# A fused two-layer block: value projections placed ahead of the first maxima, and the order of scores, maxima and layouts behind them

## The reference, cut to what matters

```
q, k, v = heads(h @ Wq + bq), heads(h @ Wk + bk), heads(h @ Wv + bv)
y  = softmax(causal(q @ k.T * scale)) @ v
qc, kc, vc = heads(h @ Wcq + bcq), heads(c @ Wck + bck), heads(c @ Wcv + bcv)
y += softmax(qc @ kc.T * scale) @ vc
x  = x + tanh(g) * (y @ Wp + bp)        # h is the layer norm of x, c the second input
```

## Time and profile before

| | |
|---|---|
| median of 3 runs | 335.41 us |
| the three runs | 332.91, 335.91, 335.41 us |
| span of the profiled execution | 337.6 us |
| mean granted clock of PE | 0.995 of full |
| PE, DVE, ACT, POOL busy | 312.9, 220.8, 194.1, 115.7 us |
| instructions | 7474 |

### The profile page before, as it was taken

One profiled execution on the slowest core, in us unless ns is written; L12 is line 12 of the kernel. 1 busy time (PEld: TensorE's weight loads), 2 busy tenths in 40 slices (PEclk: granted clock), 3 DMA queues, 4 the chain that ended last, 5 costly groups with the idle time before them and its releaser, 6 DMA issues.

```text
span 337.6 us, 7474 instructions
## 1 busy us (share of the span) xinstructions
PE 312.9 (93%) x2891; PEld 189.6 (56%) x2891; DVE 220.8 (65%) x532; ACT 194.1 (57%) x410; POOL 115.7 (34%) x200
## 2 busy tenths in 40 slices
PE   8998969989999999899977999999996899999995
PEld 3545733334443434344666677777794357776665
DVE  4998798888989889676242052333321956779665
ACT  3468588978888889787266733323336265512221
POOL 6476732327334333231775003444442211110000
PEclk9999999999999999999997999999999999999999
DMA  7855995940437006240441580000002200000101
GB/s 174 199 110 160 175 213 132 209 90 10 153 110 209 5 5 188 70 124 2 109 157 35 133 212 10 21 18 19 22 12 70 71 0 2 1 2 0 31 3 31
DMA packets 35827, 27.83 MB, mean 82 GB/s; under 512 B 5627, under 2 KB 33070, under 8 KB 35792
## 3 DMA queue, kind: packets, MB, share of 16 engines
q1 hardware_dynamic: 33965, 25.04, 29.7%
q0 software_dynamic: 1280, 1.88, 1.7%
q10 hardware_dynamic: 547, 0.44, 0.5%
HBM read 11.89 MB, written 5.26 MB: 51 GB/s over the span
## 4 chain that ended last, share of the span: by engine, by line
PE 73%; ACT 7%; DVE 6%; issue 5%; POOL 5%; DMA 2%; SPq 0%; DVEq 0%; POOLq 0%; ACTq 0%
PE psum L1682 11%; PE psum L1876 11%; PE psum L1957 8%; PE psum L1624 5%; PE psum L1648 5%; PE psum L1945 4%; PE psum L1864 4%; ACT qk_r L948 3%; PE psum L1814 2%; POOL rows_in L797 2%; PE psum L1651 2%; PE psum L2060 2%; PE psum L2052 1%; PE psum L1575 1%; PE psum L1869 1%
## 5 line engine op out<-in xcount | busy, mean ns | idle before, releaser
L1213 DVE TENSOR_REDUCE nmax<-psum 128x2 f32<-128x1024 f32 (+2 forms) x88 | 102.0, 1216 | 11.6 <-PE psum L1624 10.3
L948 ACT ACTIVATE parts<-psum 128x512 f32<-128x512 f32 (+1 forms) x88 | 45.2, 566 | 8.6 <-PE psum L1648 7.7
L1876 PE MATMUL psum<-p_more,kcat 128*128 128x320 f32 (+2 forms) x160 | 40.2, 396 | 0.9 <-DVE p_more L1346 0.7
L819 POOL DMA_INDIRECT rows_back<-qcat,back_at x24 | 22.9, 952 | 50.3 <-ACT qcat L981 43.1
L1876 PEld LDWEIGHTS psum<-p_more,kcat 128*128 128x128 f32 x160 | 26.1, 190 | 9.1 <-issue 0.9
L1350 DVE TENSOR_TENSOR qcat<-psum,qk_r 128x320 f32<-128x320 f32 (+2 forms) x40 | 16.6, 422 | 22.1 <-ACT qk_r L989 13.5
L989 ACT ACTIVATE qk_r<-psum 128x320 f32<-128x320 f32 (+2 forms) x40 | 15.2, 384 | 24.5 <-PE psum L1876 21.5
L1682 PE MATMUL psum<-parts,v_aug 128*18 128x256 f32 (+1 forms) x352 | 28.5, 369 | 0.0
L1957 PE MATMUL psum<-h_t,kcat 128*128 128x512 f32 x60 | 28.1, 594 | 0.0
L1682 PE MATMUL psum<-qk_r,v_aug 128*18 128x256 f32 (+1 forms) x160 | 27.4, 373 | 0.0
L1648 PE MATMUL psum<-qcat,kcat 64*128 64x256 bf16 x256 | 24.7, 271 | 1.9 <-ACT p_more L948 0.8
(11 more groups left out here) (249 smaller groups left out, 630.4 us busy)
## 6 DMA issues: line engine op xcount, KB each, us to landing
kcat<-parts SPq DMA_DIRECT2D x18, 192.0 KB, 3.8
qcat<-parts SPq DMA_DIRECT2D x21, 128.0 KB, 3.6
kcat<-ones_b SPq DMA_DIRECT2D x8, 192.0 KB, 4.6
kcat<-in_L_ffn_wi_gate_dram SPq DMA_DIRECT2D x6, 256.0 KB, 4.5
kcat<-in_L_ffn_wi_up_dram SPq DMA_DIRECT2D x6, 256.0 KB, 4.8
kcat<-in_L_ffn_wo_dram SPq DMA_DIRECT2D x6, 256.0 KB, 5.0
parts<-in_L_ffn_w_dram SPq DMA_DIRECT2D x3, 512.0 KB, 5.6
rows_in<-zeros SPq DMA_DIRECT2D x1, 1290.0 KB, 5.7
```

Of the source, the lines that this page charges most:

```text
L819: pool.indirect_dma_start(out=rows_back[:, :], out_offset=bass.IndirectOffsetOnAxis(ap=back_at[0:m, e, t:t + 1], axis=0), in_=eo[0:m, e % ...
L948: act.activation(p_slots[u % NPT][:, 0:w], s2_bank(s2_place[u])[:, 0:w], ACT.Exp, scale=SCALE).then_inc(p_in, 1)
L1213: dve.tensor_reduce(dst[:, :, n * g:n * (g + 1)], src.rearrange("p (r q k) -> p r q k", r=PAR, q=n), AX.X, ALU.max, negate=True).then_inc( ...
L1876: ins = pe.matmul(gate_up_bank(i, m)[:, 0:end - first], w_t[e][:, m, f * P:(f + 1) * P], xs_t[:, e % 2, first:end], start=True, stop=True)
```

## The change

`jobs` gets the values of batches 0 and 1 directly behind `ck` of batch 1, and `N_FIRST` becomes 16. 14 jobs are left, mixed with the first units. `LEAD` becomes 17. The first turn stands two units behind its part's end, not three (`FIRST_TURN_LAG`). SP loads the value weights ahead of the layouts of batch 0, on a semaphore of their own (`in_wv`). It lays out the queries of batch 1 before it waits for the batch's keys (`lay_out_split`), six and then six transfers instead of twelve in pairs. On POOL the split of the first maxima stands ahead of both subtractions of batch 3. On ACT the high part of batch 1, the clearing of gaps in `v_aug`, the bias row `bv_wide` and the third middle split change places, the last to the end of the jobs. DVE clears bank 7 before the first unit of part 1. Of the fillers 15 go (21 behind `ck` 1 and `xt` 2 out, 6 in).

```diff
-        N_FIRST = job_at("ck", 1) + 1
-        for b in range(B):
+        ahead = jobs.index(("ck", 1)) + 1
+        jobs[ahead:ahead + 1] = [("v", 0), ("cv", 0), ("xt", 2), ("v", 1), ("cv", 1)]
+        N_FIRST = job_at("cv", 1) + 1
+        for b in range(2, B):
             jobs += [("v", b), ("cv", b)]
...
-        FIRST_TURN_LAG = 3
+        FIRST_TURN_LAG = 2
...
-        LEAD = N1 + 7
+        LEAD = N1 + 6
...
+            def lay_out_split(b):
+                sp.wait_ge(early_in, 3)
+                for dst, src in lay_out_q(b):
+                    sp.dma_start(dst, src).then_inc(cat_in[b], 16)
+                sp.wait_ge(parts_in, b + 1)
+                for dst, src in lay_out_k(b, 0, KW):
+                    sp.dma_start(dst, src).then_inc(cat_in[b], 16)
...
             pad(0)
+            sp.dma_start(w_v[:, :], a["L0_xattn_Wv"]).then_inc(in_wv, 16)
+            sp.dma_start(w_cv[0:DC, :], a["L0_xattn_Wcv"]).then_inc(in_wv, 16)
+            sp.dma_start(w_cv[DC:DC + 1, :], a["L0_xattn_bcv"].unsqueeze(0)).then_inc(in_wv, 16)
...
-            lay_out_batch(1)
+            lay_out_split(SPLIT_DVE)
...
+                if b == B - 1:
+                    split_max(0)
                 pool.tensor_tensor(qk_r[:, b % 2, cols], qk[:, b % 2, cols], parts[:, b, 0, cols],
                                    ALU.subtract).then_inc(rest_in, 1)
-                if b == B - 1:
-                    split_max(0)
...
                 if (kind, i) == ("q", 2):
+                    clear_between()
                     split_middle(1)
...
-                if (kind, i) == ("v", 2):
-                    split_middle(3)
-                if (kind, i) == ("cv", 2):
+                if (kind, i) == ("v", 0):
+                    act.wait_ge(job_act, taken_count(job_at("ck", SPLIT_DVE)))
+                    take_high(SPLIT_DVE)
+                if (kind, i) == ("ct", 3):
+                    act.wait_ge(in_w, 16 * N_IN_W)
+                    act.wait_ge(zero_in, 2)
+                    act.activation(bv_wide[:, :], zeros[:, 0:D], ACT.Identity, bias=bv_col[:, :]).then_inc(wide_in, 1)
+                if (kind, i) == ("cv", 3):
                     act.wait_ge(pad_in[0], 16 * 4)
                     act.wait_ge(s1_free, turn_at[0] + 1)
                     dst, src = max_rows(0, 1)
                     act.dma_start(dst, src).then_inc(mrow_in[0], 16)
...
+            split_middle(3)
             act.wait_ge(in_w, 16 * N_IN_W)
             act.activation(tanh_g[:, :], gates[:, :], ACT.Tanh).then_inc(tanh_in, 1)
...
-            wait_taken(dve, max(j for j in range(len(jobs)) if job_bank[j] == O_BANK))
-            dve.memset(bank(O_BANK), 0.0).then_inc(o_clear, 1)
...
             for i, u in enumerate(pass1):
+                if i == N1:
+                    wait_taken(dve, max(j for j in range(len(jobs)) if job_bank[j] == O_BANK))
+                    dve.memset(bank(O_BANK), 0.0).then_inc(o_clear, 1)
...
-            UNREAD_AFTER = {("ct", 0): (2, 7), ("bias", 0): (2, 7), ("k", 0): (5, 7), ("ct", 1): (2, 2), ("ck", 1): (12, 3),
-                            ("xt", 2): (9, 3)}
+            UNREAD_AFTER = {("ct", 0): (2, 7), ("bias", 0): (2, 7), ("k", 0): (5, 7), ("ct", 1): (2, 2), ("cv", 0): (4, 7),
+                            ("v", 1): (2, 7)}
```

More of the change, by code:

```diff
@@ L243, in flamingo_gated_kernel @@
         in_w = sem("in_w")
+        in_wv = sem("in_wv")
         wide_in = sem("wide_in")
@@ L351, in flamingo_gated_kernel @@
         job_bank = [j % 8 if j < N_FIRST else JOB_RING[(j - N_FIRST) % len(JOB_RING)] for j in range(len(jobs))]
-        N_AHEAD = 1
-        N_TO_MIX = len(jobs) - N_FIRST - N_AHEAD
         def taken_count(j):
@@ L433, in flamingo_gated_kernel @@
         N_IN_LATE = 10
-        N_IN_WCK, N_IN_WQ, N_IN_W = 2, 6, 7
+        N_IN_WCK, N_IN_WQ, N_IN_W, N_IN_WV = 2, 6, 4, 3
         UNITS1 = [(s, e) for s in range(NHT) for e in range(E)]
@@ L578, in _ @@
                 sp.dma_start(dst, src).then_inc(self_in, 16)
-            for w, name in ((w_v, "Wv"), (w_p, "Wp")):
-                sp.dma_start(w[:, :], a["L0_xattn_" + name]).then_inc(in_w, 16)
+            sp.dma_start(w_p[:, :], a["L0_xattn_Wp"]).then_inc(in_w, 16)
             sp.dma_start(bv_col[:, :], a["L0_xattn_bv"].unsqueeze(1)).then_inc(in_w, 16)
-            sp.dma_start(w_cv[0:DC, :], a["L0_xattn_Wcv"]).then_inc(in_w, 16)
-            sp.dma_start(w_cv[DC:DC + 1, :], a["L0_xattn_bcv"].unsqueeze(0)).then_inc(in_w, 16)
             sp.dma_start(gates[:, 0:2], a["g_xattn"].partition_broadcast(P)).then_inc(in_w, 16)
@@ L870, in _ @@
                     act.dma_start(dst, src).then_inc(mrow_in[0], 16)
-                    act.wait_ge(in_w, 16 * N_IN_W)
-                    act.wait_ge(zero_in, 2)
-                    act.activation(bv_wide[:, :], zeros[:, 0:D], ACT.Identity, bias=bv_col[:, :]).then_inc(wide_in, 1)
                 act.wait_ge(job_done, j + 1)
@@ L907, in _ @@
                         take_high(i)
-                if (kind, i) == ("xt", SPLIT_DVE + 1):
-                    act.wait_ge(job_act, taken_count(job_at("ck", SPLIT_DVE)))
-                    take_high(SPLIT_DVE)
-                    clear_between()
+            split_middle(3)
             act.wait_ge(in_w, 16 * N_IN_W)
@@ L1563, in project @@
                     if i == 0:
-                        pe.wait_ge(in_w, 16 * N_IN_W)
+                        pe.wait_ge(in_wv, 16 * N_IN_WV)
                     for t in range(QT):
@@ L1570, in project @@
                     pe.wait_ge(wide_in, 1)
+                    pe.wait_ge(in_w, 16 * N_IN_W)
                     ins = pe.matmul(dst[:, 0:D], bv_wide[:, :], w_p[:, :], start=True, stop=True)
@@ L1704, in _ @@
             wait_taken(pe, max(j for j in range(N_FIRST) if job_bank[j] < 4))
-            for j in range(N_FIRST, N_FIRST + N_AHEAD):
-                project(j)
             done = 0
-            assert N_TO_MIX == pass1_before(0)
+            assert len(jobs) - N_FIRST <= pass1_before(0)
             while done < pass1_before(0):
@@ L1712, in _ @@
                 pass1_unit(done)
-                project(N_FIRST + N_AHEAD + done)
+                if N_FIRST + done < len(jobs):
+                    project(N_FIRST + done)
                 done += 1
```

## The result

| | before | changed |
|---|---|---|
| median of 5 runs | 333.36 us | 339.64 us |
| lowest, highest | 332.88, 335.91 | 337.53, 341.76 |
| ratio of the times | | 1.0173, 95% interval 1.012 to 1.0226 |
| span of the profiled execution | 337.6 | 340.0 |
| mean granted clock of it | 0.995 | 0.975 |

The change makes the kernel slower by 1.2 to 2.3%. The runs of the changed kernel are ordered by their clock: 337.53 us at a mean granted clock of 0.990, 339.47 at 0.983, 341.76, the profiled one, at 0.975.

A forecast was written before the change was run, and what follows sets the result against it. PE, DVE and ACT were taken as almost even, so PE's order matters. Terms 0.2 + 2.25 + 0.5 + 1.2 = +4.2 us on the 335.41 us median gave 339.6 us (341.8 for a like profile); range 334.5 to 341.8.

The forecast's parts named there:

- The middle part: Periods of twelve steps: units one step later in PE's order; early units cost 2.25 us, late units 0.5.
- The last turn: Last turn of the maxima, behind s79: its last unit comes one step later, with no room, +1.2 us.
- The maxima's transfers: Ahead of s36, s48, s60, s72: issue one step nearer the scores, landing taken as 2.3 us, no stall.
- The lead: Up to s0: work ahead of u0 costs nothing, s0 near 39.8, 2.9 us sooner; s3 to s6 only 1.2 sooner.
- Second turn and s24: Second turn, now ahead of s9: SP issues its maxima at 51.8 instead of 51.63, s24 0.2 us later.
- Nothing shrinks behind s80: After s80: PE, then POOL's row transfers, pass the delay on; no hole there shrinks from a later start.
- A: Rival, middle part: order neutral, ACT catches up within a period; between 335.4 and 336.8, say 336 us; 22%.
- B: Rival, faster: earlier lead survives, second turn 1.1 us sooner, s24 follows, middle part free; 334.3 us; 11%.
- C: Rival, middle part: maxima also late, forecast plus a stall once a period, up to 2.4 us; 341 to 342; 12%.
- D: Rival, start: loads or ACT's wait hold u0 or u9, lead not shorter, s24 hides up to 1.5 us; within forecast's 55%.

The follow-up runs named there:

- a_early1: The changed kernel with the early unit of every part but the first moved one unit sooner in its part: 339.76 us, ratio 1.0183.
- b_lead17: The kernel before with `LEAD` one smaller (17 units ahead) and two value projections instead of one ahead of u0: 340.6 us, ratio 1.019.
- a17_sp3: The changed kernel, its 17 units kept, with SP's queue in the order of b_sp3: 335.5 us, ratio 1.0013.
- a_turn1: The changed kernel with the turns of the maxima one unit sooner in their part (`TURN_LAG` = 1): 339.56 us, ratio 1.0164.
- a_sp: The changed kernel with batch 3's layouts and pads behind the third set of maxima on SP's queue, the late loads following: 344.32 us, ratio 1.0305.
- b_again: The kernel before, unchanged, run for a second profile: 334.69 us in 8 runs, ratio 1.0019.
- a_lead18: The changed kernel with `LEAD` put back, so 18 instead of 17 units run ahead: 335.24 us, ratio 1.001.
- b_sp3: The kernel before with SP's ten late loads ahead of the third set of maxima and batch 3's layouts and pads behind it: 331.87 us, ratio 0.9938.
- b_sp2: The kernel before with batch 3's layouts and pads behind the third set of maxima and the late loads behind the fourth: 342.79 us, ratio 1.0264.
- a18_sp3: The changed kernel with 18 units ahead and SP's queue in the order of b_sp3: 331.88 us, ratio 0.9924.
- a_fill: The changed kernel with nine unread 128x512 filler matmuls on zeros ahead of u0: 339.93 us, ratio 1.0154.

## Why the prediction came out right, step by step

The forecast time, 339.6, is the measured median, but that close it is by luck: two errors cancel in it. The sum said +4.2 us, and the medians differ by 6.3. The base was 335.41, of three runs, and is 333.36 of five. As a ratio I had 1.0125, near the lower end of the measured interval. That the change costs over 1% was right.

**The middle part: right.** Forecast 2.75 us over all periods, with a wait left where the early unit had been and its length added behind. The 0.47 us at s36, s48 and s60 are that wait, in every period from s36 on. From s24 to s72 I had 4 x 0.45 + 4 x 0.18 = 2.52 us; 2.07 were measured (59.46 against 57.39). a_early1 gives the early unit's share as 0.35, forecast as 0.45. The condition that I had named, that ACT's holes do not follow PE, held.

**The last turn: right in size.** With s73's early unit and the late one at s77, 0.45 - 0.18 + 1.2 = 1.47 us forecast from s72 to s84; 1.40 measured, 1.12 of them from s78 to s81 (143.29 to 148.12, against 3.71 us). The sign that I had named, PE waiting over 1 us for DVE, did not come: DVE holds it for 0.27 us, and what held the values of s78 for 0.69 us the profile does not show. PE's timeline:

```profile
144.32 0.40 PE L1693 MATMUL psum<-p_more,v_aug 128*18 128x256 f32 x2 [0.69 <-issue]
...
146.32 0.27 PE L1600 MATMUL psum<-ident_w,nmax_p 128*48 128x128 bf16 x2 [0.27 <-DVE nmax_p L1183]
```

**The maxima's transfers: right from s36 on, a stall at s12.** The waits of s36, s48, s60 and s72 are ended by ACT, none by a transfer. But s12, which the term left out, waited 0.48 us for the second set, in the changed kernel and in b_lead17. In b_lead17 that set was issued at 52.69 with its second transfer 0.8 later, and s12 started at 55.59: a landing of about 2.1 us, where I took 2.3. Where SP's queue sets s24, this wait is hidden behind it. The section of the Trainium skill that the prediction names for 2.0 us, "DMA: Bandwidth & Descriptors", Anatomy of one DMA, gives it for transfers that POOL issues, and SP issued these; for them the measured 2.1 us counts.

**The lead: right at full clock, wrong where the clock fell.** In a17_sp3, which kept the upper level to 36 us, DVE copied the first turn at 36.79 (forecast 37.0), s0 started at 39.67 (39.8), and the exponential held by POOL's last subtraction started at 42.71 (43.35). In the changed kernel's own profile these are 39.67, 42.56 and 45.59: timelines of POOL and ACT,

```profile
42.95 2.61 POOL L759 TENSOR_TENSOR parts<-qk_r,parts 128x1280 bf16<-128x1280 f32 x1 [2.12 <-ACT parts L850]
```

```profile
45.59 2.55 ACT L957 ACTIVATE qk<-psum 128x512 f32<-128x512 f32 x5 [1.10 <-POOL parts L759]
```

The mechanism is the one forecast, 2.2 to 2.8 us later. The step that failed is "PE gets four value jobs and has 15 filler matmuls fewer ... I cost all this at nothing; if the loads delayed the layouts, 0.2 us". Without the fillers PE stood idle for 1.91 us ahead of u0, and in this execution was granted 1.2 GHz for the next 7 us. It waited 1.6 to 2.5 us there in six of the eight profiles without them, 0.25 in a_turn1 and not at all in a_sp. PE at u0:

```profile
20.44 0.61 PE L1635 MATMUL psum<-kcat,qcat 64*128 64x512 bf16 x2 [1.91 <-ACT v_aug L913]
```

And u0 itself came 0.84 us later than in the first profile of before (19.60), 1.03 later than in b_again (19.41). The copy that the profile names ended at 19.43, a whole microsecond earlier; u0 asks only for the first value job's copy, done by 17.9, and for the layouts and pads of batch 0. So by the code it was one of these that landed last. SP issued the six `kcat` layouts at 10.20 us instead of 10.44, but the median from issue to landing was 3.4 us instead of 2.5, with the three weight loads issued just ahead of them. That the loads slowed them is not shown: no run moved the loads alone, and in a_turn1 and a_sp, with the same loads ahead, the median was 2.5 us again. Beyond this, the waits ahead of s0 and the clock behind them (above) stand in no term either.

**Second turn and s24: the mis-sized term.** Forecast +0.2, with bounds -1.1 and +0.6; measured +1.6 in b_lead17 and +5.1 in the changed kernel's profile. The rule behind the term held. In SP's queue the second and third sets are

```profile
56.27 1.57 SPq L631 DMA_DIRECT2D qcat<-nmax_t  x2
...
71.79 1.54 SPq L631 DMA_DIRECT2D qcat<-nmax_t  x2
```

and s24 stands 20.06 us behind the second set (76.33), where I had 19.9; in b_again it is 19.88, in b_lead17 20.09, in a_lead18 20.03. What was wrong was when the second set is issued: 51.8 forecast, 52.69 in b_lead17, 56.27 in this profile. I had let the shorter lead pay for a turn that stands one step later. In a17_sp3, whose clock stayed up to 38 us, it did pay: the second set was issued at 51.12. And I had no term for what a hole does to the clock behind it, about 1.5 us in b_lead17.

**Nothing shrinks behind s80: right**, though the two first profiles seemed to say the opposite.

**The rivals.** A (a neutral order) and B (faster) fall by the period of 14.84 us. C (the maxima's transfers late) falls in the middle part. D, that values and layouts ahead do not shorten the lead, is what the changed kernel's profile shows (s0 at 42.56; it is 39.67 in a17_sp3), but it was not hidden by s24: it moved s24.

The Trainium skill, "Perfetto Trace Analysis", Optimization Strategy, says to find what blocks a gap and to make that start sooner or end faster. Read as the prediction did for its rival, with the earlier turn, it gave 1.7 us, and that gain did not come. Applied to the real blocker of the earlier trace rows, SP's queue, it did: b_sp3 is 1.9 us faster than before. The same runs show its other half: a_sp and b_sp2 took the wait of s24 away as well and lost 4.7 and 9.4 us, against the kernels that they were made from, to what had been put further back.

## What to carry to other kernels

Where three engines are nearly even and the banks let the matmul engine run only one step ahead, put a long unit into the step that waits anyway. Shifting a whole order by one unit changed no work here and cost 14.84 against 14.32 us in each period. When a queue holds back a transfer, name for every transfer that you move behind something who waits for it and who stands behind that one, before counting the gain. Compare two profiles by the same few steps (here s24, s36, s72, s84, end) and with a second profile of the same kernel: one profile here had 5.9 us of its own. When jobs are taken out from between units, ask what the matmul engine does in that time, and look at the granted clock behind it.

The fastest versions here are b_sp3 (ratio 0.9938) and a18_sp3 (0.9924), by the order of SP's queue alone and with the change's other parts.

## What was new about the hardware

- The same wait of PE does not always bring the lower level. With 1.9 to 2.0 us of waiting ahead of u0, the granted clock fell to 0.50 in the changed kernel's profile and stayed at 1.00 in those of a_lead18 and a18_sp3. Behind the hole at s24 it fell in a_lead18 (2.13 us), a_fill (2.64) and b_lead17 (2.82), and stayed at 1.00 in a_turn1 (2.10), a_early1 (2.50) and the changed kernel (2.79).
- The changed kernel's five executions go from 337.53 us at a mean clock of 0.990 to 341.76 at 0.975.
- At the lower level a cross unit took 0.61 us (u0) instead of 0.39, and steps s3 to s9 took 9.02 us (46.73 to 55.75) in the changed kernel instead of 6.75 in a17_sp3 (43.85 to 50.60), which has the same order and ran at 1.00 from 44 us on.
- One profile of the kernel before held 5.9 us between 168 and 188 us that the next one did not have. Why is open: PE waited 2.04 us for ACT there, and 1.97 us for nothing that the profile shows.
- A DMA share of 0.91 at 209 GB/s through a whole period (b_sp3) cost PE, DVE and ACT nothing: the busy times are those of the earlier trace rows to 0.01 us.
